# Attention gather from TensorE to VectorE: masked additions, a 32x32 turn, and another order of a batch's products

## The reference

```python
x = x + xattn(layernorm(x), ctx_768, Wq, bq, Wk, bk, Wv, bv, Wo, bo)
# xattn: 64 batches, 16 heads of 16 channels, 32 queries, 257 keys
q = (query @ Wq + bq)            # scaled by 16 ** -0.5
k = (key_value @ Wk + bk)
v = (key_value @ Wv + bv)
attn = softmax(clip(q @ k.T, -10000, 10000))
out = (attn @ v).reshape(B, 32, 256) @ Wo + bo
```

## Time and profile before

| | |
|---|---|
| median of 3 runs | 675.95 us (675.88 to 678.5) |
| the profiled execution | 677.32 us, span 675.5 us |
| attention, start of the first to start of the last batch's scores | 18.65 to 373.88 us |
| next stage, first product | 385.35 us |
| busy share of the span | TensorE 93%, VectorE 70%, ScalarE 51%, GpSimd 51% |
| mean granted TensorE clock | 0.974 |

### The profile page before, as it was taken

One profiled execution on the slowest core, in us unless ns is written; L12 is line 12 of the kernel. 1 busy time (PEld: TensorE's weight loads), 2 busy tenths in 40 slices (PEclk: granted clock), 3 DMA queues, 4 the chain that ended last, 5 costly groups with the idle time before them and its releaser, 6 DMA issues. The chain is left out here.

```text
span 675.5 us, 17938 instructions
## 1 busy us (share of the span) xinstructions
PE 626.1 (93%) x6540; PEld 515.8 (76%) x6540; DVE 474.5 (70%) x1072; ACT 341.1 (51%) x743; POOL 342.9 (51%) x482
## 2 busy tenths in 40 slices
PE   7999999999999999999999899988799999993677
PEld 3777888887888878888888678876378888882566
DVE  3685777876678867776777585688879987773344
ACT  3655777776777656666666344644033233331111
POOL 3455688875878765567775233213133333215551
PEclk9999999999999999999999999989699999996899
DMA  9734374884765977121210199004934434435664
GB/s 236 165 89 105 96 239 149 265 206 160 225 213 170 270 210 175 35 65 33 66 33 2 34 426 384 33 33 163 343 109 134 135 125 141 127 107 160 188 194 114
DMA packets 57909, 104.02 MB, mean 154 GB/s; under 512 B 5952, under 2 KB 40960, under 8 KB 56800
## 3 DMA queue, kind: packets, MB, share of 16 engines
q1 hardware_dynamic: 52528, 88.58, 42.0%
q0 software_dynamic: 4432, 13.50, 7.2%
q10 hardware_dynamic: 864, 0.79, 0.5%
HBM read 71.59 MB, written 31.26 MB: 152 GB/s over the span
## 5 line engine op out<-in xcount | busy, mean ns | idle before, releaser
L640 ACT ACTIVATE Pm<-Pm,nm 128x257 f32<-128x257 f32 x256 | 116.6, 507 | 92.7 <-DVE nm L534 92.7
L529 DVE TENSOR_SCALAR Pm<-scores 128x514 f32<-128x514 f32 x128 | 87.9, 687 | 68.9 <-PE scores L733 68.8
L534 DVE TENSOR_REDUCE nm<-Pm 128x2 f32<-128x514 f32 x128 | 88.2, 689 | 4.4
L762 PEld LDWEIGHTS bank<-Vs,PT 128*64 128x64 f32 x2048 | 65.0, 138 | 26.2 <-issue 26.2
L714 PE MATMUL bank<-hA,wH 128*128 128x258 f32 x256 | 84.3, 330 | 0.0
L744 PE MATMUL bank<-cst,Pm 128*128 128x128 f32 x512 | 77.8, 275 | 4.1 <-ACT kT L618 4.0
L1628 POOL DMA_INDIRECT Xg<-y_d,inv x39 | 37.2, 954 | 87.1 <-PE scores L1813 69.8
L434 POOL TENSOR_TENSOR Mb<-Os,rc 128x128 f32<-128x128 f32 x64 | 26.1, 408 | 104.9 <-DVE rc L554 104.2
L721 PE MATMUL bank<-wH,hA 128*128 128x256 f32 x256 | 75.6, 307 | 0.0
L762 PE MATMUL bank<-Vs,PT 128*64 128x33 f32 x2048 | 72.0, 224 | 1.7 <-DVE OT L558 1.4
L714 PE MATMUL bank<-hA,wL 128*128 128x258 f32 x256 | 72.1, 282 | 0.0
(11 more groups left out here) (262 smaller groups left out, 1476.8 us busy)
## 6 DMA issues: line engine op xcount, KB each, us to landing
w_d<-whl SPq DMA_DIRECT2D x16, 1024.0 KB, 6.1
W<-w_d SPq DMA_DIRECT2D x8, 2048.0 KB, 15.3
g_d<-gg SPq DMA_DIRECT2D x39, 256.0 KB
wst<-in_W1T SPq DMA_DIRECT2D x16, 512.0 KB, 6.6
cx<-in_ctxT SPq DMA_DIRECT2D x31, 258.0 KB, 2.9
cx<-in_ctxT SPq DMA_DIRECT2D x62, 129.0 KB, 3.5
bb<-in_b SPq DMA_DIRECT2D x8, 512.0 KB, 12.7
Vt<-vx_d SPq DMA_DIRECT2D x6, 528.0 KB, 10.0
```

The costliest lines, as they stand in the source:

```text
L529: v.tensor_scalar(Pm[:, i % 2, 2 * p:2 * p + 2, :], S4[:, 2 * p:2 * p + 2, 0:NK], -CLAMP, CLAMP, ALU.max, ALU.min).then_inc(s_cl, 1)
L534: v.tensor_reduce(nm[:, i % 2, 2 * p:2 * p + 2], Pm[:, i % 2, 2 * p:2 * p + 2, :], AX.X, ALU.max, negate=True).then_inc(s_nm, 1)
L640: a.activation(Pm[:, i % 2, g, :], Pm[:, i % 2, g, :], ACT.Exp, bias=nm[:, i % 2, g:g + 1]).then_inc(s_ex, 1)
L762: mm = t.matmul(pO[r, VC * g:VC * g + VC], PT[:, i % 2, p, 2 * gg + c, r], Vs[:, i % 4, c, 4 * h + g, :], start=first, stop=(c == 1), skip ...
```

## The change

The weighted sum's 34 columns are now two sets of 17, one for each head of a pair: 16 channels and a weight sum. `total` takes them with two masked additions: `Oh` = first set * mask of the even head + tail part, `Os` = second set * mask of the odd head + `Oh`. So a row keeps only its own head. `Os`, the tail part and `Mb` shrink to 68, 68 and 64 elements. `gather` and the constant `R2` are gone: `otevac` turns 32x32 blocks of `Mb` straight into `OT` on VectorE. The order of heads (`head_order`) is other, and the rows of `Wo` follow it. The tail rows `Vt` are loaded for each 32 partitions apart, four transfers for two, each half as wide.

The order of work changes too. On TensorE both transpositions come right behind the weighted sum, and then both key projections and the values in one run. `uses` follows. On VectorE `ptevac` stands between the second `clip` and the second `negmax`; on ScalarE `ptevac` comes first in the turn. The two filler products at the end are gone, and the loop has one turn less.

```diff
-VC = 33
+VH = 17
+VC = 2 * VH
...
-            for p in range(2):
-                if i + 1 < T:
-                    uses += [(("k", i + 1, p), s_ke, 2 * (i + 1) + p + 1)]
-                if 1 <= i:
-                    uses += [(("p", i - 1, p), s_pte[p], i)]
+            if 1 <= i:
+                uses += [(("p", i - 1, p), s_pte[p], i) for p in range(2)]
+            if i + 1 < T:
+                uses += [(("k", i + 1, p), s_ke, 2 * (i + 1) + p + 1) for p in range(2)]
...
-                    for h in range(2):
-                        sp.dma_start(Vt[64 * h:64 * h + 64, first:first + n, :, :].rearrange("p t a b -> p t (a b)"),
+                    for r in range(4):
+                        sp.dma_start(Vt[32 * r:32 * r + 32, first:first + n, :, :].rearrange("p t a b -> p t (a b)"),
...
                 def norm(i):
 
                     g.wait_ge(s_rc, i + 1)
                     if i >= 2:
-                        g.wait_ge(s_o, i)
-                    g.tensor_tensor(Mb[:, i % 2, :, :, :],
-                                    Os[:, i % 2, :, 0:32].rearrange("p g (h c) -> p h g c", h=2),
-                                    rc[:, i % 2, :].unsqueeze(1).unsqueeze(3).broadcast_to([128, 2, 4, 16]), ALU.mult
+                        g.wait_ge(s_ote, i - 1)
+                    g.tensor_tensor(Mb[:, i % 2, :, :], Os[:, i % 2, :, 0:16],
+                                    rc[:, i % 2, :].unsqueeze(2).broadcast_to([128, 4, 16]), ALU.mult
...
-                    v.tensor_tensor(Os[:, i % 2, :, :].rearrange("p a b -> p (a b)"), pO[:, 0:4 * VC],
-                                    tm[:, i % 2, :, :].rearrange("p a b -> p (a b)"), ALU.add).then_inc(s_oa, 1)
+                    parts = pO[:, 0:4 * VC].rearrange("p (g s c) -> p g s c", g=4, s=2)
+                    v.scalar_tensor_tensor(Oh[:, i % 2, :, :], parts[:, :, 0, :], om[:, 0:1], tm[:, i % 2, :, :],
+                                           ALU.mult, ALU.add).then_inc(s_oh, 1)
+                    v.wait_ge(s_oh, i + 1)
+                    v.scalar_tensor_tensor(Os[:, i % 2, :, :], parts[:, :, 1, :], om[:, 1:2], Oh[:, i % 2, :, :],
+                                           ALU.mult, ALU.add).then_inc(s_oa, 1)
...
                 def otevac(i):
-                    v.wait_ge(s_o, i + 2)
-                    v.tensor_copy(OT[:, :, :].rearrange("p m (b t) -> p m b t", t=T)[:, :, :, i],
-                                  pO[:, 256:320].rearrange("p (m q) -> p m q", m=2)).then_inc(s_ote, 1)
+                    v.wait_ge(s_m, i + 1)
+                    v.transpose(OT[:, :, :].rearrange("p m (b t) -> p m b t", t=T)[:, :, :, i],
+                                Mb[:, i % 2, :, :].rearrange("p (m g) c -> p m (g c)", m=2)).then_inc(s_ote, 1)
...
-                        for p in range(2):
-                            clip(i, p)
-                            negmax(i, p)
+                        clip(i, 0)
+                        negmax(i, 0)
+                        clip(i, 1)
+                        if i >= 1:
+                            ptevac(i - 1)
+                        negmax(i, 1)
...
                 for i in range(-1, T + 1):
+                    if 1 <= i:
+                        ptevac(i - 1)
                     if 0 <= i < T:
                         exps(i, 0)
                         exps(i, 1)
                     if i + 1 < T:
                         kevac(i + 1, 0)
-                    if 1 <= i:
-                        ptevac(i - 1)
-                    if i + 1 < T:
                         kevac(i + 1, 1)
...
-                def gather(i):
-                    if i == T - 1:
-                        t.wait_ge(s_cl, 2 * T)
-                        busy(1)
-                    t.wait_ge(s_m, i + 1)
...
                     if 2 <= i < T + 2:
-                        mm = weigh(i - 2)
-                    if i >= 3:
-                        mm = gather(i - 3)
-                    if i >= 2:
-                        mm.then_inc(s_o, 1)
-                    for p in range(2):
-                        if i + 1 < T:
-                            kproj(i + 1, p)
-                        if 1 <= i <= T:
+                        weigh(i - 2)
+                    if 1 <= i <= T:
+                        for p in range(2):
                             transp(i - 1, p)
                     if i + 1 < T:
+                        for p in range(2):
+                            kproj(i + 1, p)
                         vproj(i + 1)
```

More of the change, by code:

```diff
@@ L72, in tile_rows @@
     return c
-def head_rows():
-    p = np.arange(128)
-    r = np.zeros((128, 2, 2, NQ), np.float32)
-    for hh in range(2):
-        for half in range(2):
-            r[:, hh, half, :] = (((p // 64 == half) & ((p // 32) % 2 == hh))[:, None]
-                                 & (p[:, None] % 32 == np.arange(NQ)))
-    return r.reshape(128, 2, 2 * NQ)
 def head_order():
-    half, g, hh, dd = np.meshgrid(np.arange(2), np.arange(4), np.arange(2), np.arange(16), indexing="ij")
-    return (half * 128 + g * 32 + hh * 16 + dd).transpose(0, 2, 1, 3).reshape(-1)
+    j, half, hh, gl, dd = np.meshgrid(*(np.arange(n) for n in (2, 2, 2, 2, 16)), indexing="ij")
+    return (half * 128 + (2 * j + gl) * 32 + hh * 16 + dd).reshape(-1)
 def build(nc, d, out, vx_d, w1_d, y_d, g_d):
@@ L228, in build @@
         lA = put("lA", [128, 2, 2, NKP], F32R)
[L229 to L232 removed]
+        Vt = put("Vt", [128, T, 4, VH])
+        tm = put("tm", [128, 2, 4, VH])
+        Oh = put("Oh", [128, 2, 4, VH])
+        Os = put("Os", [128, 2, 4, VH])
+        Mb = put("Mb", [128, 2, 4, 16])
         rc = put("rc", [128, 2, 4])
@@ L513, in _ @@
                 v.wait_ge(s_v1, 1)
-                v.tensor_copy(vx[:, :, :, 0:32], held("x")[0:T, 0:C].rearrange("p (a g c) -> p a g c", g=4, a=2)
-                              ).then_inc(s_vxe, 1)
+                for h in range(2):
+                    v.tensor_copy(vx[:, h, :, :, 0:16],
+                                  held("x")[0:T, 128 * h:128 * h + 128].rearrange("p (g s c) -> p s g c", g=4, s=2)
+                                  ).then_inc(s_vxe, 1)
                 qevac(0)
@@ L810, in _ @@
                 t.wait_ge(s_wl, 1)
-                for i in range(-1, T + 3):
+                for i in range(-1, T + 2):
                     if 0 <= i < T:
```

80 lines of the change are left out of this document (29 added, 51 removed).

## The result

The changed kernel took 660.34 us (659.23 to 661.76, four runs) against 675.91 us before on the same chip, a ratio of 0.977 with an interval of 0.974 to 0.980: 15.6 us or 2.3% faster, inside the range and 5.8 above the forecast of 654.5. The profiled execution took 661.8 us with a span of 659.2, 16.3 less than the span before.

What follows compares the result with a forecast made beforehand. TensorE's own work was taken to bound the attention: 62 batches at 0.33 us less give 20.5, plus 1.0 at the end, 21.5 off 675.95, hence 654.5 us; range 647 to 665.

Steps and rivals of the forecast that it cites:

- The sum per batch: TensorE's attention batch: gather and two run heads go, transpositions cost 0.08 more; 5.37 becomes 5.04 us, 0.33 less.
- a head at the upper end: Between weighted sum and transpositions: an extra 0.10 us, counted only in the slowest case, a batch of 5.17.
- What bounds the kernel: In the attention: TensorE's own work, without a hole, sets the batch time of 5.37 us.
- its two sums: The new TensorE batch added step by step, 5.04 us, and by subtracting savings from 5.37, 5.00 us.
- Covers: Time left before a late copy delays TensorE: VectorE 0.35, ScalarE 0.25 and 0.2, GpSimd 0.7 us.
- the rule that the prediction weighed: VectorE: minimize the operation count; eight become nine a batch, adding about 0.3 us inside 0.9 spare.
- (1): GpSimd's low half or ScalarE's bank comes late in the attention; batch 5.20, total about 665; chance 0.16.
- (3): VectorE's additions and turn at their upper ends make its round about 5.29, total 670; chance 0.07.
- (2): More gain on TensorE: eight transpositions at 0.80 and no head, batch 4.90, total 646; chance 0.08.
- Normalizations: Batches behind VectorE's query normalizations: TensorE stands 1.2 us before the values instead of 1.00; no change counted.
- The end: Last scores to next stage's first product: 11.47 becomes 10.5 us, saving 1.0.
- the clock's fall: After TensorE stands at the attention's end: the granted clock drops, costing 1.7 us; put at even odds.

Runs made afterwards that it cites:

- e3: The kernel before with only the new order of work on TensorE, VectorE and ScalarE, gather kept on TensorE; 658.3 us, ratio 0.989.
- e2: The changed kernel with the old order of work on TensorE, VectorE and ScalarE, leaving only the gather's move to VectorE; 667.55 us, ratio 1.001.
- e9: The kernel before with only ScalarE reordered: first key copy and transposed-half copy moved ahead of the second exponential; 668.33 us against 677.3, ratio 0.985.
- e7: The changed kernel with the old order, but ScalarE's first key copy and transposed-half copy ahead of its second exponential; 654.48 us in one run against 665.57.
- e10: The changed kernel with eight more, unread 32x32 turns of Mb on VectorE in each batch; 672.78 us in one run against 677.3.
- e8: The changed kernel with VectorE's copy of the second transposed half behind the second maximum instead of ahead of it; 673.74 us in one run against 665.57.
- e6: The changed kernel with four filler products at the attention's end and query normalizations spread over three turns; 643.85 us, ratio 0.968.
- e11: The changed kernel with query normalizations spread over three turns, without filler products; 655.38 us against 676.37, ratio 0.967.
- e5: The changed kernel unchanged, run again on another chip; 648.7 us against 665.57 for the kernel before, ratio 0.975.
- e4: The changed kernel with the eight transpositions ahead of the weighted sum, in all batches but the last turns; 658.25 us, ratio 0.989.
- e1: The changed kernel with two filler products in each of the two places where TensorE stands at the attention's end; 647.4 us against 666.58, ratio 0.972.
- e12: The changed kernel with both spread normalizations and four filler products, run once more; 651.96 us against 676.37, ratio 0.965.

## Why the prediction was right, and where it was not

The forecast came out in time and in most of its steps, but its account of what a batch waits for was wrong, and two errors from it nearly cancelled. That the total came so close is in part luck.

**The sum per batch** was 0.33 less and measured 0.29, 5.08 for 5.04. Step by step, forecast and measured: scores 0.62 and 0.62; weighted sum 0.95 and 1.06; transpositions 0.88 and 0.85; run of 20 with what follows 2.59 and 2.55. The mis-sized term is the weighted sum: its 34th column cost nothing, as forecast, but the border to the transpositions behind it costs 0.11 (1.06, where it took 0.96 ahead of the gather in e3), and I had it only as a head at the upper end. 62 times 0.04 is 2.5 us; the batch from the second scores to the third gave 0.62 (5.39 to 4.77) instead of 0.33 and won a little back.

**What bounds the kernel** was the step that failed in its reasoning, though not in the sum. The prediction said: "TensorE's own row of work sets the time of a batch", and one batch is "without a hole". That is not what e2 and e9 show. Of the second transpositions' 0.44 and the head behind them some 0.10 were the price of a bank that ScalarE gave back late: e9 moves its copies forward and has 0.36. No row carries a wait; only the 0.36 of the first four beside the 0.44 of the second hinted at it, and I read both as the cost of transpositions. The table behind the earlier trace rows also has a wait that I passed over: ScalarE for VectorE's maxima, 70.8 us in 50 times, a link of this very string. The ledger, each entry a difference of two kernels:

| from 5.37 | a batch | shown by |
|---|---|---|
| ScalarE's copies out of the way | -0.10 | before, e9 |
| gather gone, 0.25, less the border 0.11 | -0.14 | e9, e7 (one run) |
| two heads less, eight transpositions in a run | -0.05 | e7, after |
| | 5.08 | |

The prediction had the gather at its full 0.25, and 0.08 for the rest (0.20 of heads less 0.08, less the 0.04 between its two sums). In its place came 0.14 and 0.15. Two wrong sizes nearly cancelled, by luck. Had the change been the gather alone, the same working would have promised 0.25 a batch, and e2 measured nothing.

**Covers** (the time between an engine's end and the moment when another needs it). They held in quiet batches, as argued. VectorE: additions 0.28 and 0.29 (forecast 0.28), turn drawn at 0.27 (0.24), spare forecast 0.9, 1.0 by e10. The copy's cover was forecast 0.35, some 0.3 by e8. The Trainium skill's page VectorE: DVE Perf Modes says under "Rules for kernel authors", beside the rule that the prediction weighed, that the 32x32 transposition is fastest on VectorE. The trace agrees as far as the two ways here go: the turn holds VectorE 0.13 us in e10's run of eight, while the gather, which turned on TensorE, was worth 0.14 to 0.25 of that engine. The weight load comes late to ScalarE only three times in 260 us, by up to 0.8 (0.3 to 0.5 forecast), and the quiet batches stay at 5.08.

Of the rivals, (1) covers too thin and (3) VectorE as the bound didn't come; e8 shows (1) at work when the copy sits one place later. Two of their sums don't come out of their own terms: with additions of 0.48 and a turn of 0.69 VectorE's round in (3) is 3.14 + 0.52 + 0.52 + 0.09 + 0.73 = 5.00, not 5.29, and would not have been the bound; the batch of (2) is 4.96 less a head of 0.10, 4.86, not 4.90. Neither enters the forecast.

**Normalizations.** Forecast a wait of 1.2 at the values instead of 1.0 elsewhere, no change in sum; measured 1.05, 0.92 and 0.93, the batch 6.39 for 6.60. Right, and e6 and e11 show that spreading the work takes the wait away: 6.39 became 5.08.

**The end.** Forecast 10.5, and the clock's fall at even odds for 1.7. e5 took 10.37, so the chain was sized well. The fall at the next stage came in all eight profiles of kernels without filler products (the changed kernel, e2, e4, e5, e7, e8, e10, e11): the head takes 9.4 to 10.3 us there, and 7.9 in the six with them. Between the changed kernel and the one before that is 1.7 (9.59 and 7.91). So even odds were too low. What I had left out is a first fall, behind the stand of 1.95 us: in the profiled execution the end took 11.83, in e11 and e10 11.49. So in place of a gain of 1.0 the end lost 0.4 and then 1.7.

Sum for the profiled execution: 18.6 for the batches (forecast 20.5), 1.0 by the earlier first scores (not the change's), -0.4 at the end (forecast 1.0) and -1.7 in the head are 17.5; the span is 16.3 shorter, and the 1.2 between, in the later stages, was not looked into.

## What to carry to other kernels

Before a product is taken off a full engine, follow the longest string of the other engines from the same start to each of its bank uses: where the product starts at the same 0.05 us behind the string's end in every batch, it waits, though the engine looks full, and the saving has nowhere to go (e2) until the string is cut. The cut may be one call moved, at no cost (e9). Two halves of a change can be worth 0.00 and 0.15 apart and 0.29 together, so a half that measures nothing isn't refuted. Once covers are thin, spread lumps of side work over several turns, and when filler work is taken out, ask what kept the clock up.

## What the runs showed of the hardware

- The weighted sum (32 short products, 64 stationary columns) costs 0.11 us more ahead of products with 128 stationary columns (1.06 against 0.95), and fp32 transpositions of 128 columns cost 0.17 more ahead of the weighted sum (1.02 against 0.85, e4). The scores, with 64 columns too, take 0.63 ahead of the transpositions and 0.62 ahead of the weighted sum. So the change of width alone doesn't cost it; what does was not tried.
- The first key or value product behind anything else costs 0.08 to 0.11 us more than one inside the run (0.20 to 0.23 to the next, against 0.12).
- A product of TensorE that waits for a copy of ScalarE's starts 0.05 to 0.06 us behind the copy's end (the values in 41 batches of the kernel before). The profile's table of waits doesn't list this wait, because the transpositions ahead of the values are drawn to last beyond the values' start (205.08 and 0.62 against 205.52).
- Equal stands did not have equal effects. In the end of the attention, behind 1.95 us of stand at the same place, the granted clock went to its lower level of 1.2 GHz in the changed kernel's first profile (0.66 on average from 358 to 362), in e10 and in e11, and stayed at 2.4 GHz in e5. In e2 it stayed up behind a stand of 1.32, in e7 it fell behind the same stand (0.52 on average from 364 to 368). With two fillers in each stand it stayed up in e1, e6 and e12.
- A 32x32-block turn of 128x64 fp32 is drawn 0.25 to 0.27 us long, and one follows the other after 0.13.
- The kernel before took 666 us on some chips and 676 to 677 on others. The changed kernel's profiled executions took 661.8 and 646.0 (e5), with the next stage's first product at 366.1 and 364.5; so 13 of these 16 us lie behind it. The cause was not looked for.
